# Layer 1's flag product ahead of the last chunk, transposed scores paired to 512 columns, GpSimd given a third tile, and 128-row scores in layer 0

## The chip, the cores and the metric

One core of one Trainium2 chip runs the whole program in one launch. The metric is the device time in microseconds, the median of several runs. Beside it stands one execution taken with the hardware profiler, whose lines are shown here. Line numbers such as L1502 are lines of the kernel before.

## The reference

Two transformer layers on an input of 2 batches x 1024 tokens x 128 features. Each normalizes the rows and then adds an attention and a feed-forward part to its input:

```python
xn = layernorm(x); x = x + attn0(xn) + ffn0(xn)      # layer 0
xn = layernorm(x); x = x + attn1(xn) + ffn1(xn)      # layer 1
```

`attn0` has 16 heads of 8 features, with biases, causal mask and softmax. `ffn0` is a mixture of 8 experts with the best two chosen. `ffn1` walks 8 decision trees of depth 7. `attn1` has 16 query heads and 4 key heads of 64 features, with rotary positions, causal mask and a choice of the 64 largest scores of each row:

```python
scores = einsum('bhqd,bhkd->bhqk', q, k) / 8; scores = where(future, -1e30, scores)
threshold = top_k(scores, 64)[0][..., -1:]
weights = softmax(where(scores < threshold, -1e30, scores))
out = einsum('bhqk,bhkd->bhqd', weights, v) @ Wo.T
```

## The kernel before

The program runs stage after stage: projections of layer 0, its attention (`attend_layer0`, about 80 to 547 us), its experts, projections of layer 1, the trees, and layer 1's attention (`attend_layer1`, from about 1215 us to the end). Each stage has a block of code for every engine, and semaphores order them. The order of the work on each engine is written out by hand. P is 128, S is 1024 rows of a batch, TB = 8 tiles of 128 rows, and CH = 512 columns.

**Layer 0, one head (32 of them, software pipelined).** For a stable softmax the kernel first needs each row's peak. `row_unit` computes scores row by row (line 350, operands of 64 rows, and a mask of 128 rows, line 353) in 12 units of at most 512 columns into two buffers; VectorE reduces each unit to a maximum (line 463) and makes from the maxima three bf16 parts of a shift (lines 466 to 472). TensorE turns the shift (line 394), ScalarE copies it into rows 64 to 66 of `q` (line 439), where `k` holds ones. Then the scores are computed again with keys on the partitions (line 407, 128 rows, with a mask, line 410), one tile of keys at a time, ScalarE takes the exponential (line 445), and `pv` multiplies by the values of the head before (line 374). ScalarE copies that product (`oT`, line 451) behind the exponential of tile 5, and TensorE transposes it into the row buffers (line 424). `rows_ahead(count)` issues row units of the next head between these steps: two at first, then 2, 1, 2, 1, 1, ... behind each tile of keys. GpSimd copies values (`values`).

**Layer 1, one section.** A section n works on several heads at once: it computes the scores of head n+1, counts in head n, sorts head n-1, weighs head n-2 and leaves head n-3. The sections n = 4 to 27 run as six turns of a loop of four; the others are written out.
- TensorE, `scores`: a tile of 128 rows against all its keys in fp32 (line 1208) and a mask (line 1210). VectorE's `keep_scores(j)` copies it to SBUF with its peak (line 1463). `TILE` turns j into the tile, the widest first: j = 0 is 1024 columns, j = 7 is 128.
- ScalarE, `count`: three times, it counts the scores above a trial value in every tile (line 1332). Between them VectorE works out the next trial from the count in small steps (`first_move`, ends in line 1548; `second_move`, ends in line 1581). They are split by `yield`, so that other work is put between the steps.
- VectorE, `tally` and `split_tally` (lines 1421 to 1430): from the three counts, a value `found` slightly above the threshold. `mark(i)` keeps of tile i what lies below it (line 1436, two SBUF inputs). GpSimd does this for tiles 7 and 6 by a comparison (line 1307) and a product (line 1312), `EARLY = 2`. `sort(i, 0..2)` takes the sixteen largest of what is left by three passes (lines 1448, 1450, 1452). Behind the sorting, eight small steps make the threshold, and a `verdict` whether the search failed somewhere in the head.
- The flag: TensorE sums the verdict over the partitions (line 1260), VectorE copies it (`flags`, line 1470), loads it into a register and branches (`judge`); behind that it writes the `cutoff` (line 1502). Where the flag is set the head's tiles are sorted in full.
- ScalarE, `gate` (line 1342): per tile, a large number where a score lies under the cut-off. TensorE, `turn` (lines 1224, 1226): a chunk of up to four 128x128 blocks is transposed and the gate subtracted, into one of two buffers. ScalarE, `weights` (line 1351): the exponential of the chunk. TensorE, `weigh` (line 1237): times the values.
- ScalarE copies the sum (`copy_out`, line 1358), TensorE projects it (`project`, line 1249), VectorE divides and adds it to `x` (`shares`, line 1510, and `leave`, line 1519).

The lines of the flag on TensorE stand at the head of a section, behind all chunks of the section before:

```python
if gating:
    pe.wait_ge(verdict_ready, n - 1)
    wait(pe, t_read, (n - 2) * TU)
    pe.matmul(ps_flag, g.ones[:, 0:1], verdict[:, :], start=True, stop=True).then_inc(flag_back, 1)
```

## Time and profile before

| what | value |
|---|---|
| time, median of 3 runs | 2691.27 us (2687.34 to 2691.73) |
| the profiled execution's own time | 2691.92 us |
| its span in the profile | 2689.9 us |
| mean granted clock of TensorE | 0.858 of full speed |
| busy: TensorE, VectorE, ScalarE, GpSimd | 77%, 64%, 53%, 15% |
| TensorE's weight loads | 43% |

The span runs from the first to the last instruction; the time has 2.0 us more around it. Busy shares are means over stages that differ, so they don't say what bounds one stage. The granted clock has two levels, 1.2 GHz (0.5) and 2.4 GHz (1.0).

### The profile page before, as it was taken

What the parts mean: (1) busy time and instruction counts of PE and PEld (TensorE: products, weight loads), DVE (VectorE), ACT (ScalarE), POOL (GpSimd) and SP (SyncE); (2) the same over time, 40 slices, a digit from 0 to 9 for tenths busy, and PEclk for the clock granted to TensorE, in tenths of its full rate; (3) what the DMA queues carried; (4) which work ended last, traced back from release to release, by engine and by line L of the source; (5) the groups of instructions that cost most, each with busy time, mean ns of one, the idle gap of its engine ahead of it and who ended that gap; (6) DMA issues with size and microseconds to landing.
All of it is one profiled execution on the core that took longest, in us unless ns stands there. A gap on an engine that the chain in (4) does not pass through costs nothing. (4 is left out here: it accounts for less than half of the span.)

```text
span 2689.9 us, 36464 instructions
## 1 busy us (share of the span) xinstructions
PE 2060.2 (77%) x10416; PEld 1158.8 (43%) x10448; DVE 1710.9 (64%) x4622; ACT 1415.4 (53%) x2979; POOL 393.6 (15%) x262
## 2 busy tenths in 40 slices
PE   6799999899988968885676777777767567767766
PEld 4233333377764435552343444444434334434434
DVE  4556656521125666765886777777777777877784
ACT  2344444444324213324766666666666566766673
POOL 0000000000012400001212121222212212221211
PEclk7699999999968969997788878788888778888877
DMA  6000000000011200001000000000000000000000
GB/s 179 18 16 15 15 15 15 8 28 1 0 39 55 88 15 0 0 5 44 21 13 25 13 25 12 25 12 24 14 24 17 20 12 18 19 24 12 17 5 21
DMA packets 38267, 62.43 MB, mean 23 GB/s; under 512 B 10226, under 2 KB 15348, under 8 KB 38005
## 3 DMA queue, kind: packets, MB, share of 16 engines
q1 hardware_dynamic: 38069, 60.51, 7.7%
q14 instruction: 161, 1.31, 0.2%
q8 instruction: 37, 0.61, 0.1%
HBM read 34.14 MB, written 17.83 MB: 19 GB/s over the span
## 5 line engine op out<-in xcount | busy, mean ns | idle before, releaser
L1332 ACT ACTIVATE a_trash<-a_sc,a_search 128x1024 bf16<-128x1024 f32 (+7 forms) x768 | 585.7, 766 | 294.2 <-DVE a_search L1581 164.4
L1237 PE MATMUL a_ps_o<-a_kT,a_v 128*65 128x512 f32 (+3 forms) x768 | 376.8, 584 | 214.8 <-ACT a_kT L1351 213.6
L1208 PE MATMUL a_ps_s<-a_k,a_q 128*128 128x512 f32 (+3 forms) x768 | 343.5, 562 | 141.5 <-DVE a_sc L1463 128.1
L1307 POOL TENSOR_SCALAR a_below<-a_sc,a_found 128x1024 f32<-128x1024 f32 x64 | 171.9, 2686 | 1103.5 <-POOLq L1303 1103.5
L1224 PE MATMUL a_ps_t<-g_ident,a_sc 128*128 128x128 f32 x1152 | 298.2, 331 | 33.4 <-ACT a_short L1342 33.3
L463 DVE TENSOR_REDUCE a_top<-a_ps_row 128x1 f32<-128x512 f32 (+3 forms) x384 | 207.4, 557 | 161.4 <-PE a_ps_row L353 107.6
L1226 PE MATMUL a_ps_t<-a_minus,a_short 128*128 128x128 bf16 x1152 | 268.0, 253 | 0.0
L1224 PEld LDWEIGHTS a_ps_t<-g_ident,a_sc 128*128 128x128 f32 x1152 | 199.2, 173 | 154.9 <-issue 92.0
L1351 ACT ACTIVATE a_kT<-a_ps_t 128x512 f32<-128x512 f32 (+3 forms) x384 | 184.6, 481 | 118.8 <-PE a_ps_t L1226 115.0
L1208 PEld LDWEIGHTS a_ps_s<-a_k,a_q 128*128 128x128 f32 x768 | 142.2, 214 | 235.9 <-DVE a_sc L1463 140.5
L445 ACT ACTIVATE a_prob<-a_ps_col 128x1024 f32<-128x1024 f32 (+7 forms) x256 | 158.3, 653 | 147.2 <-PE a_ps_col L407 113.0
L1342 ACT ACTIVATE a_short<-a_sc,a_cutoff 128x1024 bf16<-128x1024 f32 (+7 forms) x256 | 177.0, 764 | 95.3 <-DVE a_cutoff L1502 95.1
L1463 DVE TENSOR_SCALAR_CACHE_REDUCE a_sc<-a_ps_s,g_search 128x1024 f32<-128x1024 f32 (+7 forms) x256 | 207.2, 809 | 24.6 <-PE a_ps_s L1210 9.0
L1237 PEld LDWEIGHTS a_ps_o<-a_kT,a_v 128*65 128x65 f32 x768 | 88.7, 158 | 285.6 <-ACT a_kT L1351 238.0
L1448 DVE MAX8 a_sorted<-a_below 128x8 f32<-128x768 f32 (+7 forms) x256 | 192.8, 754 | 1.2
L1452 DVE MAX8 a_sorted<-a_below 128x8 f32<-128x768 f32 (+7 forms) x256 | 192.5, 752 | 0.0
L1450 DVE MATCH_REPLACE8 a_below<-a_sorted,a_below 128x768 f32<-128x768 f32 (+7 forms) x256 | 189.5, 742 | 0.0
L1226 PEld LDWEIGHTS a_ps_t<-a_minus,a_short 128*128 128x128 bf16 x1152 | 139.8, 121 | 91.6 <-issue 91.5
L584 ACT ACTIVATE ex_hid<-ex_ps_h,le_b 128x512 f32<-128x512 f32 x128 | 87.8, 687 | 128.5 <-PE ex_ps_h L561 128.1
L1332 ACT ACTIVATION_READ_ACCUMULATOR a_trash<-a_sc,a_search 128x1 f32 x768 | 147.0, 191 | 0.0
L350 PE MATMUL a_ps_row<-a_k,a_q 64*128 64x512 bf16 (+3 forms) x384 | 132.5, 346 | 13.9 <-DMA a_k<-stack 12.7
L1312 POOL TENSOR_TENSOR a_below<-a_sc,a_below 128x1024 f32<-128x1024 f32 x64 | 142.4, 2225 | 2.8
(244 smaller groups left out, 3218.3 us busy)
## 6 DMA issues: line engine op xcount, KB each, us to landing
a_v<-g_v SPq DMA_DIRECT2D x32, 260.0 KB, 2.3
q1turned<-p_full SPq DMA_DIRECT2D x32, 256.0 KB, 2.0
a_q<-q1turned SPq DMA_DIRECT2D x32, 256.0 KB, 3.6
a_k<-k1turned SPq DMA_DIRECT2D x32, 256.0 KB, 4.1
stack<-p_parts SPq DMA_DIRECT2D x24, 256.0 KB, 3.8
a_q<-stack SPq DMA_DIRECT2D x32, 96.0 KB, 2.2
a_k<-stack SPq DMA_DIRECT2D x32, 96.0 KB, 2.2
le_w<-d_w SPq DMA_DIRECT2D x1, 2048.0 KB, 8.9
```

What stands on the lines that cost most here:

```text
L463: m = dve.tensor_reduce(top[:, i, c:c + 1], ps_row[:, u % 2, 0:width], AX.X, ALU.max)
L1208: pe.matmul(ps_s[:, j % 2, c:c + w], q[:, p, i * P:width], k[:, p, c:c + w], start=True, stop=True)
L1224: pe.matmul(out, columns(h, i)[:, c * P:(c + 1) * P], g.ident[:, :], is_transpose=True, start=True, stop=False)
L1226: m = pe.matmul(out, short[:, OFF[i] + c * P:OFF[i] + (c + 1) * P], minus[:, :], start=False, stop=True)
L1237: m = pe.matmul(ps_o[0:VW1, lo // HALF, (lo % HALF) * P:CH], v[:, p, c, :], kT[:, x % 2, 0:(hi - lo) * P], start=(c == 0), stop=(c == hi - 1))
L1332: act.activation(trash[:, u % 2, 0:(i + 1) * P], columns(h, i), ACT.Sign, scale=-1.0, bias=trials[:, p, c, i:i + 1], accum_out=balance[:, ...
L1342: act.activation(short[:, OFF[i]:OFF[i] + (i + 1) * P], columns(h, i), ACT.Relu, scale=-STEEP, bias=cutoff[:, h % 2, i:i + 1]).then_inc(ga ...
L1351: act.activation(kT[:, x % 2, 0:w], ps_t[:, x % 2, 0:w], ACT.Exp).then_inc(t_read, 1)
L1448: m = dve.max(sorted_[:, i, 0:8], buf)
L1450: m = dve.match_replace(buf, sorted_[:, i, 0:8], buf, -3.0e38)
L1452: m = dve.max(sorted_[:, i, 8:16], buf)
L1463: dve.tensor_scalar(columns(h + 1, i), ps_s[:, j % 2, 0:(i + 1) * P], shift.rearrange("p n i -> p (n i)"), None, ALU.subtract, ALU.max, ac ...
```

## The change

In layer 0, the row scores take all 128 rows of `q` and `k` instead of the first 64. Since rows 64 to 66 of `q` hold an old shift by then, GpSimd clears them behind each head's last columns (`clear`, 1024 columns of three partitions), and TensorE waits for it. Behind every tile of keys two row units are issued, so that the twelve end with tile 4, before its `pv`.

In layer 1:
- The product of the flag moves from the head of section n+1 to the end of section n, ahead of the last `weigh`, and to the buffer that is free there.
- The 12 chunks become 9 of 512 columns: narrow pieces are put together, and their order changes. The gates are made all in one go, the small tiles first.
- TensorE's scores j = 4 to 7 of the next head are issued behind chunks 0, 1, 3 and 5 instead of 0, 1, 2 and 3, the two of the head after that behind chunks 6 and 7. `scores(7)` so stands behind `weigh(5)` and `turn(7)`.
- `EARLY = 3`: GpSimd marks tile 5 too.
- VectorE's order: the first two kept scores and `mark(4)` come between tally and flag, `mark(3)` between the flag and its branch, `mark(2)` behind the cut-off; tile 5 is sorted last, tiles 7, 6, 1 and 0 earlier, and `keep_scores(7)` comes behind `sort(5, 0)`.

```diff
@@ attend_layer0
+                def clear(n, h):
+                    pool.wait_ge(v_ready, n + 2)
+                    pool.wait_ge(col_ready, n * CU + CU)
+                    pool.tensor_tensor(q[SHIFT0:SHIFT0 + NSH, h, :], none[SHIFT0:SHIFT0 + NSH, :],
+                                       none[SHIFT0:SHIFT0 + NSH, :], ALU.add).then_inc(cleared, 1)
+                    pool.wait_ge(cleared, n + 1)
...
-                with pool.Fori(1, NH // 2) as i:
-                    values(i * 2, 0)
-                    values(i * 2 + 1, 1)
+                with pool.Fori(1, NH // NQ) as i:
+                    for h in range(NQ):
+                        clear(i * NQ + (h - 2), (h + 2) % NQ)
+                        values(i * NQ + h, h % 2)
...
+                        wait(pe, cleared, i4 * NQ + (h - NQ + 1))
...
-                    last = pe.matmul(ps_row[:, u % 2, 0:width], q[0:SHIFT0, h, i * P:(i + 1) * P],
-                                     k[0:SHIFT0, h, c * CH:c * CH + width], start=True, stop=True)
+                    last = pe.matmul(ps_row[:, u % 2, 0:width], q[:, h, i * P:(i + 1) * P],
+                                     k[:, h, c * CH:c * CH + width], start=True, stop=True)
...
-                        rows_ahead(2 if j in (0, 2) else 1)
+                        rows_ahead(2)
...
+                dve.memset(none[:, :], 0.0)
@@ attend_layer1
-        EARLY = 2
+        EARLY = 3
...
-        CHUNKS = [(c, max(c, lo), lo + HALF) for lo in (HALF, 0) for c in range(lo + HALF)]
+        CHUNKS = ([((0, 0, 4),), ((1, 1, 4), (3, 3, 4))] + [((c, HALF, TB),) for c in range(5)]
+                  + [((5, 5, 8), (7, 7, 8)), ((6, 6, 8), (2, 2, 4))])
+        NARROW = 2
+        LAST = (2, 6)
+        GATES = [0, 1, 2, 3, 7, 6, 5, 4]
...
@@ TensorE
-                    if gating:
-                        pe.wait_ge(verdict_ready, n - 1)
-                        wait(pe, t_read, (n - 2) * TU)
-                        pe.matmul(ps_flag, g.ones[:, 0:1], verdict[:, :], start=True, stop=True).then_inc(flag_back, 1)
...
                     for x in range(TU):
+                        if sorting and x == TU - 1:
+                            pe.wait_ge(verdict_ready, n)
+                            pe.matmul(ps_t[0:1, 1 - odd, 0:TB + 1], g.ones[:, 0:1], verdict[:, :], start=True,
+                                      stop=True).then_inc(flag_back, 1)
                         if gating:
-                            weigh(n - 2, i4 * 2 + h // 2 - 1, h % 2, x)
+                            weigh(n - 2, i4 * 2 + h // 2 - 1, h % 2, odd + x, x)
                             if x + 2 < TU:
-                                turn(n - 2, h + 2, x + 2)
-                        if ahead and x < HALF:
-                            scores(n + 1, i2, p1, HALF + x)
-                        if late and x in (9, 11):
-                            scores(n + 2, i4 * 2 + (h + 2) // 2, 1 - p1, x // 2 - 4)
+                                turn(n - 2, h + 2, odd + x, x + 2)
+                        if ahead and x in (0, 1, 3, 5):
+                            scores(n + 1, i2, p1, HALF + (x + 1) // 2)
+                        if late and x in (6, 7):
+                            scores(n + 2, i4 * 2 + (h + 2) // 2, 1 - p1, x - 6)
@@ ScalarE
-                        if leaving and s == 1:
+                        if leaving and s == 2:
                             copy_out(n - 3)
                     if gating:
-                        for j in range(HALF):
+                        for j in range(TB):
                             gate(n - 2, h + 2, j)
...
-                            weights(n - 2, s // 2)
-                    if gating:
-                        for j in range(HALF, TB):
-                            gate(n - 2, h + 2, j)
-                        weights(n - 2, HALF)
+                            weights(n - 2, odd + s // 2, s // 2)
+                    if gating:
+                        weights(n - 2, odd + HALF, HALF)
...
-                            weights(n - 2, HALF + 1 + s // 2)
-                    if gating:
-                        for x in range(2 * HALF + 1, TU):
-                            weights(n - 2, x)
+                            weights(n - 2, odd + HALF + 1 + s // 2, HALF + 1 + s // 2)
```

VectorE's order in a full section after the change, `next` being one step of a move:

```python
tally; split_tally; keep_scores(0), (1); mark(4); flags; mark(3); judge; cut_off
next(first); mark(2); next(first); shares(0); next(first); shares(1); leave(0)
rest of first; leave(1); keep_scores(2); mark(1); sort(4,0); mark(0); sort(3,0), (4,1), (3,1)
shares(2); leave(2); keep_scores(3); sort(4,2), (2,0), (3,2), (2,1), (7,0), (2,2); keep_scores(4)
sort(7,1), (1,0), (7,2), (1,1), (6,0); next(second); sort(6,1); next(second); keep_scores(5)
next(second); sort(1,2); next(second); sort(0,0); next(second); sort(0,1); next(second); sort(0,2)
rest of second (line 1581); keep_scores(6); sort(6,2), (5,0); keep_scores(7); sort(5,1); hit; sort(5,2)
eight small steps to the verdict
```

## Rows read from the trace of the kernel before

**Rows 1.** Layer 1's attention: busy us (instructions) by engine, clock, DMA
```profile
1215.00:2690.00 1475.00, 1019.77 (x4672) 587.31 (x4672) 1096.15 (x3186) 962.90 (x2241) 317.05 (x158) 0.82 0.07 18
```

**Rows 2.** Groups by line, 1379.5 to 2089.4 us; then all of line 439
```profile
L1502 DVE SCALAR_TENSOR_TENSOR a_cutoff<-a_thr,a_ceiling 128x8 f32<-128x8 f32 x16 | 2.9, 179 | 38.5 <-issue 38.5
...
L439 ACT ACTIVATE a_q<-a_ps_col x32: 1012/1012/1012, 92.2 to 520.1; 3x1024 bf16<-3x1024 f32 x32
```

**Rows 3.** VectorE's timeline, layer 1: start, duration, what, [idle before <-releaser]
```profile
1723.41 0.18 DVE L1421 TENSOR_TENSOR a_above<-a_wide,a_balance 128x24 f32<-128x24 f32 x1 [2.96 <-remote]
...
1728.66 0.15 DVE L1470 TENSOR_SCALAR a_flag<-a_ps_t 1x1 int32<-1x1 f32 x1 [4.24 <-PE a_ps_t L1260]
...
1757.59 0.16 DVE L1581 SCALAR_TENSOR_TENSOR a_search<-a_fac,a_search 128x8 f32<-128x8 f32 x1
...
1765.42 0.18 DVE L1421 TENSOR_TENSOR a_above<-a_wide,a_balance 128x24 f32<-128x24 f32 x1
...
1771.93 0.15 DVE L1470 TENSOR_SCALAR a_flag<-a_ps_t 1x1 int32<-1x1 f32 x1 [5.50 <-PE a_ps_t L1260]
1772.38 1.28 DVE L1463 TENSOR_SCALAR_CACHE_REDUCE a_sc<-a_ps_s,g_search 128x1024 f32<-128x1024 f32 x1 [0.31 <-issue]
...
1773.93 1.15 DVE L1463 TENSOR_SCALAR_CACHE_REDUCE a_sc<-a_ps_s,g_search 128x896 f32<-128x896 f32 x1 [0.26 <-DVE a_sc L1463]
...
1777.42 0.17 DVE L1502 SCALAR_TENSOR_TENSOR a_cutoff<-a_thr,a_ceiling 128x8 f32<-128x8 f32 x1 [2.33 <-issue]
```

**Rows 4.** Groups of VectorE by line and shape in layer 1, 1400 to 2400 us
```profile
L1450 DVE MATCH_REPLACE8 a_below<-a_sorted,a_below 128x1024 f32<-128x1024 f32 x23 | 27.8, 1209 | 0.0
...
L1436 DVE SCALAR_TENSOR_TENSOR a_below<-a_sc,a_found 128x768 f32<-128x768 f32 x22 | 22.2, 1010 | 0.0
```

**Rows 5.** Timeline of ScalarE in the same section of layer 1
```profile
1757.86 1.15 ACT L1332 ACTIVATE a_trash<-a_sc,a_search 128x1024 bf16<-128x1024 f32 x1 [5.19 <-DVE a_search L1581]
...
1760.04 0.47 ACT L1351 ACTIVATE a_kT<-a_ps_t 128x384 f32<-128x384 f32 x1
...
1764.65 0.20 ACT L1332 ACTIVATION_READ_ACCUMULATOR a_trash<-a_sc,a_search 128x1 f32 x1
```

**Rows 6.** TensorE's timeline, layer 1; last, a stretch with its clock (0.58)
```profile
1787.66 1.44 PE L1237 MATMUL a_ps_o<-a_kT,a_v 128*65 128x512 f32 x2 [4.59 <-ACT a_kT L1351]
...
1790.17 1.82 PE L1208 MATMUL a_ps_s<-a_k,a_q 128*128 128x512 f32 x2
...
1799.55 0.49 PE L1208 MATMUL a_ps_s<-a_k,a_q 128*128 128x128 f32 x2 [1.75 <-DVE a_sc L1463]
...
1787.60:1791.50 3.90, 3.84 (x12) 1.96 (x13) 3.87 (x10) 3.90 (x11) 0.00 (x0) 0.58 0.00 0
```

**Rows 7.** GpSimd's timeline, behind the tally of 1765.42
```profile
1766.62 2.84 POOL L1307 TENSOR_SCALAR a_below<-a_sc,a_found 128x1024 f32<-128x1024 f32 x1 [32.02 <-POOLq L1303]
...
1769.58 2.35 POOL L1312 TENSOR_TENSOR a_below<-a_sc,a_below 128x1024 f32<-128x1024 f32 x1
```

**Rows 8.** Timelines at 1297 us; all of line 1502, ns min/median/max
```profile
1297.48 2.34 DVE L1436 SCALAR_TENSOR_TENSOR a_below<-a_sc,a_found 128x640 f32<-128x640 f32 x1
...
1297.07 2.08 POOL L1312 TENSOR_TENSOR a_below<-a_sc,a_below 128x896 f32<-128x896 f32 x1
...
L1502 DVE SCALAR_TENSOR_TENSOR a_cutoff<-a_thr,a_ceiling x32: 166/168/686, 1294.4 to 2658.3; 128x8 f32<-128x8 f32 x32
```

**Rows 9.** Timeline of TensorE in one head of layer 0
```profile
303.72 0.39 PE L350 MATMUL a_ps_row<-a_k,a_q 64*128 64x512 bf16 x1
304.04 0.23 PE L353 MATMUL a_ps_row<-g_maskq,g_identb 128*128 128x128 bf16 x1
...
305.20 0.39 PE L407 MATMUL a_ps_col<-a_q,a_k 128*128 128x512 bf16 x1
305.43 0.22 PE L410 MATMUL a_ps_col<-g_maskk,g_identb 128*128 128x128 bf16 x1
```

**Rows 10.** Groups by line and shape in layer 0, 110 to 520 us
```profile
L463 DVE TENSOR_REDUCE a_top<-a_ps_row 128x1 f32<-128x512 f32 x180 | 124.5, 692 | 47.3 <-PE a_ps_row L350 44.0 <-PE a_ps_row L353 0.4
```

More of the change, by code:

```diff
@@ L1212, in scores, with turn, weigh @@
                     m.then_inc(s_ready, 1)
[L1214 to L1216 removed]
+                def turn(n, h, u, x):
                     if x == 0:
                         pe.wait_ge(gated, n * TB + HALF)
[L1219 removed]
+                    if x == NARROW:
                         pe.wait_ge(gated, n * TB + TB)
                     wait(pe, t_read, n * TU + (x - 1))
[L1222 to L1227 removed]
+                    a = 0
+                    for c, lo, hi in CHUNKS[x]:
+                        for i in range(lo, hi):
+                            out = ps_t[:, u % 2, a * P:(a + 1) * P]
+                            pe.matmul(out, columns(h, i)[:, c * P:(c + 1) * P], g.ident[:, :], is_transpose=True,
+                                      start=True, stop=False)
+                            m = pe.matmul(out, short[:, OFF[i] + c * P:OFF[i] + (c + 1) * P], minus[:, :],
+                                          start=False, stop=True)
+                            a += 1
                     m.then_inc(t_ready, 1)
[L1230 to L1232 removed]
+                def weigh(n, n2, p, u, x):
                     if x == 0:
@@ L1252, in section @@
                 def section(n, i4, h):
-                    ahead, _, _, gating, leaving = parts_of(n)
+                    ahead, _, sorting, gating, leaving = parts_of(n)
                     late = not isinstance(n, int) or n + 2 < NH
@@ L1469, in flags @@
                         dve.wait_ge(flag_back, n - 1)
-                        return did(dve.tensor_scalar(flag[:, TB:TB + 1], ps_flag[:, TB:TB + 1], float(TB * P), None, ALU.add))
+                        return did(dve.tensor_scalar(flag[:, TB:TB + 1], ps_t[0:1, p, TB:TB + 1], float(TB * P), None, ALU.add))
                     def do_again(i):
@@ L1492, in judge @@
                             dve.sem_clear(redo)
-                            Chain(dve, redo)(dve.tensor_scalar(flag[:, 0:TB], ps_flag[:, 0:TB], float(P), None, ALU.add))
+                            Chain(dve, redo)(dve.tensor_scalar(flag[:, 0:TB], ps_t[0:1, p, 0:TB], float(P), None, ALU.add))
                             do_again(0)
@@ L1594, in section @@
                         keep_scores(1)
+                    if sorting:
+                        mark(4)
+                    if gating:
+                        flagged = flags()
+                    if sorting:
+                        mark(3)
                     if gating:
@@ L1598, in section @@
                         cut_off()
+                    next(first, None)
+                    if sorting:
+                        mark(2)
+                    next(first, None)
                     if leaving:
                         shares(0)
+                    next(first, None)
+                    if leaving:
                         shares(1)
                         leave(0)
+                    for _ in first:
+                        pass
+                    if leaving:
                         leave(1)
-                    if sorting:
-                        mark(5)
-                    next(first, None)
                     if ahead:
                         keep_scores(2)
-                    next(first, None)
                     if sorting:
-                        mark(4)
-                    next(first, None)
-                    if sorting:
-                        mark(3)
-                    next(first, None)
+                        mark(1)
+                        sort(4, 0)
+                        mark(0)
+                        sort(3, 0)
+                        sort(4, 1)
+                        sort(3, 1)
                     if leaving:
@@ L1618, in section @@
                         leave(2)
-                    if sorting:
-                        mark(2)
-                        sort(5, 0)
-                        mark(1)
-                        sort(4, 0)
-                        mark(0)
-                    for _ in first:
-                        pass
-                    if sorting:
-                        sort(5, 1)
-                        sort(4, 1)
                     if ahead:
@@ L1651, in section @@
                     if sorting:
-                        sort(2, 2)
-                    next(second, None)
-                    if sorting:
-                        sort(1, 0)
+                        sort(1, 2)
                     next(second, None)
@@ L1660, in section @@
                     if sorting:
-                        sort(1, 1)
+                        sort(0, 1)
+                    next(second, None)
+                    if sorting:
+                        sort(0, 2)
                     for _ in second:
                         pass
-                    if sorting:
-                        sort(7, 2)
                     if ahead:
```

72 lines of the change are left out of this document (34 added, 38 removed).

## The prediction

> **What bounds the kernel now.** I read first what the busy times of layer 1's attention say: it takes 1475 of 2690 us, and no engine fills it; VectorE, the fullest, has 1096 us, TensorE 1020 [rows 1]. The groups of lines then give the rhythm: 16 sections (heads) of layer 1 in 709.9 us, 44.4 us each, and 32 heads of layer 0 at (520.1 - 92.2) / 31 = 13.8 us, mostly 13.5 [rows 2].
>
> What closes the loop in layer 1 is in VectorE's timeline. It tallies a head at 1765.42, and then stands 5.5 us for the flag's product (4.24 in the section before, beside a 2.96 us loop branch) [rows 3]. TensorE issues that product only after the last chunks and two large scores, and those chunks wait for ScalarE's third count, which starts 0.27 us after VectorE's second move (line 1581) [rows 3, 5]. So the ring is: flag to second move, 1728.66 to 1757.59 = 28.9 us of VectorE's own work, then 1757.59 to 1771.93 = 14.3 us through ScalarE and TensorE; 43.3 us, and about 1 us more a section from loop branches.
>
> **Layer 1, the new ring.** With the product ahead of the last `weigh`, VectorE meets no wait after the tally. Time from tally (T) to the second move, starting from the 28.9:
> - the flag stood 0.45 ahead of the first kept score [rows 3]; now tally and split come first (1.0, the row of line 1307 starting 1.20 after the tally shows when `found` is out [rows 3, 7]) and 0.45 of registers: +1.0;
> - `mark(5)` goes to GpSimd: -1.05 [rows 4];
> - tile 5's three passes move behind the second move: 3 x 0.9, -2.7; ahead of it come the third pass of tile 7 (1.15), two of tile 6 (2.1), and small passes of tiles 1 and 0 (0.35 and 0.5): +4.1. The passes of 1024 columns are 1.21 [rows 4], the others are scaled by width, less 0.07 of overlap;
> - kept score to cut-off is 1777.42 - 1773.93 = 3.49 [rows 3], of which the kept score covered 1.15; `mark(3)` (0.75) covers less: +0.5 with the flag's copy.
> Sum 28.9 + 1.0 - 1.05 - 2.7 + 4.1 + 0.5 = 30.8; I carry 30.9.
>
> From the second move to the next tally, before: 7.8 [rows 3]. Now `keep_scores(7)` stands there, and score 7 is issued after `weigh(5)` and `turn(7)`. `weigh(5)` needs ScalarE's fifth-indexed weights, after two counts: 1760.04 - 1757.59 = 2.45 [rows 3, 5], 0.6 for a chunk of 512, then `weigh` and `turn` of four tiles, 1790.17 - 1787.66 = 2.5 at the clock's lower level [rows 6], and a score of 128 columns, 0.8 after its start (0.49 at the upper level [rows 6]). That is 6.4 after the move; VectorE's own work in between is 2.4, so a new stall of about 4. Behind it stand `sort(5,1)`, `hit`, `sort(5,2)` and the eight small steps to the next tally (0.3 + 0.9 + 0.2 + 1.0 + 1.8 = 4.2). Total 10.6. TensorE will be at the lower level there: it has been idle some 7 us by then, and after a shorter idle of 4.6 us the granted clock was 0.58 over the next 3.9 us [rows 6].
>
> ScalarE's counts end 1764.85 - 1757.59 = 7.3 after the move [rows 3, 5], 8.1 with four chunks of 512 between: under 10.6, so the stall for score 7 covers them. The product itself is out about 2 to 3 us after T (TensorE does two large scores first), and VectorE asks at 4.8: covered, by 2 us. Without that cover its wait comes back. Pairing 12 chunks to 9 changes no column and saves ScalarE three short instructions, hidden; so are the eight gates in one go, since by my count the second tally that VectorE asks for is then complete at T + 22 and asked for at T + 27.
>
> The loop branch of 2.96 [rows 3] now lies wholly on VectorE's path: 0.73 a section. For moments at which TensorE's two large scores run at the lower clock I add 0.35.
> Section: 30.9 + 10.6 + 0.73 + 0.35 = 42.6, a gain of 1.8 on 44.4, if VectorE runs undisturbed.
>
> **What GpSimd's third tile costs.** Before, nearly all marks run after GpSimd is done. Where they do meet, a mark of 128x640 took 2.34 us, more than twice one of 128x768 (1.01), and ended 0.67 after GpSimd's TENSOR_TENSOR; the cut-off, ordinarily 0.17, took up to 0.69 in such a spot [rows 4, 8]. I read that as: a VectorE instruction with two SBUF inputs stands until GpSimd's TENSOR_TENSOR ends. The Trainium skill (GPSIMD Engine Reference, Key points) says the same, that the engines share SBUF interfaces and contend for VectorE instructions with two SBUF inputs; by that rule the new order pays, without it the gain of 1.8 stands.
>
> GpSimd's times after T are 1.2 to 4.0 compare, 4.2 to 6.5 multiply [rows 7], then compare and multiply to 11.2, and for tile 5 (scaled to 768 columns) compare to 13.4, multiply to 15.3. VectorE: `mark(4)` at 4.1, `mark(3)` 4.9, cut-off 8.4, `mark(2)` 8.7, line 1545 at 9.7, line 1548 at 11.1, `mark(1)` 14.1, `mark(0)` 15.2. If `mark(4)` gets in 0.1 us ahead of the first multiply, GpSimd shifts by 0.7; `mark(3)` then stands, but the branch before the cut-off hides that; line 1548 or 1545 stands 0.85 to 2.1, `mark(1)` or `mark(0)` 0.9 to 1.3: 2.0 to 2.9, taken 2.3. All lie ahead of the second move, on the ring. Section 44.9, +0.5. About 30 sections run in full: +15 us. The first and last sections, and the one redo, I cost at nothing: same work.
>
> **Layer 0.** At 512 columns, a 64-row score takes 304.04 - 303.72 = 0.32 to the next instruction, a 128-row one 305.43 - 305.20 = 0.23 [rows 9]. So each change between 64 and 128 rows costs 0.09 to 0.10; 12 row units have 24 of them, 2.3 us a head. Most of it isn't kept. `rows_ahead(2)` puts all twelve units ahead of the third `pv`, at the rate at which VectorE reduces (0.69 for 512 columns [rows 10]): I count 1.2 us of new waits at tiles 2 and 4. The third `pv`, and with it tile 5's columns and the copy of `oT`, come at nearly their old place in the head, and the transposes that follow set its end. Kept 0.4 a head, 31 x 0.4 = 12 us; bounds 0.3 lost and 1.4 kept. GpSimd's `clear` has no row; by its 1024-column instruction [rows 7] it takes 2.3, below that 0.25 if three partitions were cheap. It starts after the head's last columns and GpSimd is otherwise idle; uncovered, it would hold VectorE's shift and cost up to 0.8 a head. The extra memset is 0.5 us, once.
> The Trainium skill (TensorE: Matmul & The Clock Gate, Part 3) says a weight load overlaps a running matmul only if its row group differs. By that, 128 rows throughout would expose every load and layer 0 would gain nothing, 12 us more in the sum. The rows of 128 rows disagree: 0.23 us for 512 columns leaves a load no room [rows 9].
>
> **Sum.** Own time of the profiled execution 2691.9 (span 2689.9 plus 2.0): +15 - 12 + 0.5 = 2695.4; it lies 0.6 above the runs' median, so 2695.
>
> **Rivals.**
> 1. No contention worth naming (few cases in the trace; the races fall well). 30 x -1.8 = -54, -12: 2626. For it: marks beside GpSimd's compare ran at their usual time. Against: the 2.34 us mark. It decides from a loss under 1.8 a section. Chance 0.27.
> 2. `mark(4)` loses the race for GpSimd's first multiply: it stands 2.4, the branch and the cut-off start that much later, line 1548 still meets a multiply. 4.0 lost a section, +2.2 x 30 = +66, -12: 2746. The two arrive within 0.1 us. Chance 0.20.
> 3. TensorE at its upper clock after the wait (5.2 in place of 6.4), or layer 0 keeping over 1 us a head: 2655 to 2675. Chance 0.08. Layer 0's `clear` on VectorE's path: 2720, chance 0.02. Layer 0 giving nothing at all, because the gap of 0.09 us isn't one of rows: 2707, inside the forecast, 0.05 of its chance; the two gaps at equal width speak against it [rows 9].
> The forecast (2675 to 2715) has 0.43.
>
> **Chances.** 0.2% is 5.4 us, about what can be told from no change. The forecast's own range gives 0.11 faster, 0.12 same, 0.20 slower. With the rivals: faster 0.27 + 0.07 + 0.11 = 0.45, same 0.13, slower 0.42. To hold 8 in 10 the range takes in rivals 1 and 2: 2620 to 2750.
>
> **What the profile would show.** Right: no wait of line 1470; about 4 us of idle before `keep_scores(7)`, put down to TensorE; two-input VectorE instructions stretched where GpSimd multiplies; sections of 44 to 46 us. Marks at their old means and sections of 42.6 mean rival 1; a `mark(4)` of 3 us means rival 2. In layer 0, row scores 0.23 apart at 512 columns and heads near 13.1. I am wrong if the stall before `keep_scores(7)` isn't there, or if contention hits the sorting passes too.

## Result, and the profile after

The changed kernel takes 2763.59 us (median of 4 runs, 2762.1 to 2765.5) against 2691.45 for the kernel before: ratio 1.0272, 95% interval 1.0254 to 1.0290. It is slower, by 70.2 us between the two profiled executions (2762.1 and 2691.9), and outside the predicted range. Among the runs below one execution of `both`, 4619.5 us where its nine others took 2682 to 2689, is left out.

Where it goes is seen from three rows. The first is all of the line that copies layer 0's shift rows, once a head (line 439 before, [rows 2]); the second all of layer 1's kept scores; the third the row of layer 1's attention that answers to [rows 1].

```profile
L455 ACT ACTIVATE a_q<-a_ps_col x32: 1012/1012/1012, 91.5 to 501.3; 3x1024 bf16<-3x1024 f32 x32
...
L1481 DVE TENSOR_SCALAR_CACHE_REDUCE a_sc<-a_ps_s,g_search x256: 334/810/1286, 1199.9 to 2650.8; 128x1024 f32<-128x1024 f32 x32, 128x768 f32<-128x768 f32 x32, 128x512 f32<-128x512 f32 x32, 128x256 f32<-128x256 f32 x32
...
1190.70:2760.20 1569.50, 1029.71 (x4672) 594.99 (x4672) 1226.41 (x3154) 950.28 (x2145) 464.80 (x222) 0.77 0.06 17
```

Layer 0 gained: its 32 heads run from 91.5 to 501.3, 409.8 us in place of 427.9 [rows 2]. Layer 1 lost more than that: its kept scores take 1450.9 us from first to last, 95.3 more than before (1224.3 to 2579.9 there). In the third row VectorE is busy for 1226 us, 130 more than in [rows 1], although the change moved work from it to GpSimd, whose busy time rose from 317 to 465.

VectorE's timeline shows one section of it, as [rows 3] does for before. It starts with the kept score of the smallest tile, at the end of the section before. Columns: start, duration, what, and in brackets the idle time before it and its releaser.

```profile
1872.44 0.35 DVE L1481 TENSOR_SCALAR_CACHE_REDUCE a_sc<-a_ps_s,g_search 128x128 f32<-128x128 f32 x1 [4.53 <-PE a_ps_s L1228]
...
1876.63 0.18 DVE L1439 TENSOR_TENSOR a_above<-a_wide,a_balance 128x24 f32<-128x24 f32 x1
...
1880.73 3.09 DVE L1454 SCALAR_TENSOR_TENSOR a_below<-a_sc,a_found 128x640 f32<-128x640 f32 x1
1883.75 0.14 DVE L1488 TENSOR_SCALAR a_flag<-a_ps_t 1x1 int32<-1x1 f32 x1
1883.82 1.43 DVE L1454 SCALAR_TENSOR_TENSOR a_below<-a_sc,a_found 128x512 f32<-128x512 f32 x1
1887.60 0.80 DVE L1520 SCALAR_TENSOR_TENSOR a_cutoff<-a_thr,a_ceiling 128x8 f32<-128x8 f32 x1 [2.35 <-issue]
...
1888.39 1.27 DVE L1454 SCALAR_TENSOR_TENSOR a_below<-a_sc,a_found 128x384 f32<-128x384 f32 x1
...
1891.41 1.06 DVE L1566 SCALAR_TENSOR_TENSOR a_search<-a_fac,a_search 128x8 f32<-128x8 f32 x1
```

And GpSimd's timeline of the same section:

```profile
1880.79 2.36 POOL L1336 TENSOR_TENSOR a_below<-a_sc,a_below 128x1024 f32<-128x1024 f32 x1
1883.13 3.09 POOL L1331 TENSOR_SCALAR a_below<-a_sc,a_found 128x896 f32<-128x896 f32 x1
1886.30 2.07 POOL L1336 TENSOR_TENSOR a_below<-a_sc,a_below 128x896 f32<-128x896 f32 x1
1888.35 2.20 POOL L1331 TENSOR_SCALAR a_below<-a_sc,a_found 128x768 f32<-128x768 f32 x1
1890.63 1.81 POOL L1336 TENSOR_TENSOR a_below<-a_sc,a_below 128x768 f32<-128x768 f32 x1
```

The wait for the flag is gone: line 1488 has no idle time before it. In its place the instructions of VectorE that read two operands from SBUF and lie beside GpSimd's multiplies are long. `mark(4)`, 640 columns, starts 0.06 us ahead of the multiply and ends 0.67 behind it; the cut-off of 8 columns ends 0.03 behind the second multiply, line 1566 0.03 behind the third. Kept scores, which read PSUM, keep their duration. `keep_scores(7)` has the new wait that the prediction speaks of, 4.53 us.

To compare runs I take the same numbers from each trace: from VectorE's tally (T) to its next one, over the full sections between about 1400 and 2620 us (23 to 26 of them, without the one that is redone; which of the last sections are counted moves a mean by up to 0.3), and in it T to the flag, T to the cut-off, T to the second move, and second move to next tally. "Excess" is, summed over VectorE's instructions of a section, what each takes above its usual time, that of the same line and shape in early0, where GpSimd marks nothing, so that early0 has 0.00 by definition. "Branch" is from the end of the branch ahead of the cut-off to the cut-off's start. All are means in us.

```
kernel       section  flag   cut-off  2nd move  rest   excess  branch
before        44.23   6.75   12.26    35.82      8.41   0.04    2.80
changed       47.67   6.99   10.73    35.98     11.69   5.12    2.89
early0        45.91   4.84    9.43    34.12     11.79   0.00    3.54
early2        45.92   6.87   10.64    34.16     11.77   3.53    2.84
late          47.65   4.07    8.69    36.01     11.65   2.97    3.67
late_dl       46.40   4.06    7.69    34.96     11.43   2.95    2.67
sc7           44.06   7.12   11.48    35.79      8.27   2.96    3.45
both          44.45   5.42    9.37    36.17      8.28   2.62    3.06
sc7_dl        43.81   7.24   10.85    35.56      8.25   3.07    2.75
sc7_e2_dl     42.51   7.20   10.77    34.07      8.44   2.03    2.72
best          41.40   7.04   10.59    32.96      8.44   1.69    2.69
flag          43.11   4.78   11.50    34.72      8.39   0.09    3.98
```

### The profile page after: what moved, and what is told of

Same layout as the page of the kernel before. It is cut to its first block and busy times, and to the rows that moved or that the text cites. A ratio compares the mean times of both kernels' runs of the same rounds, so it can differ in the third digit from the quotient of the medians.

```text
span 2760.2 us, 36380 instructions
## 1 busy us (share of the span) xinstructions
PE 2007.9 (73%) x10448; PEld 1154.2 (42%) x10448; DVE 1837.0 (67%) x4591; ACT 1403.8 (51%) x2883; POOL 600.3 (22%) x356
## 5 line engine op out<-in xcount | busy, mean ns | idle before, releaser
L1331 POOL TENSOR_SCALAR a_below<-a_sc,a_found 128x1024 f32<-128x1024 f32 (+2 forms) x96 | 257.8, 2686 | 1054.6 <-POOLq L1327 1054.6
L1373 ACT ACTIVATE a_kT<-a_ps_t 128x512 f32<-128x512 f32 x288 | 169.0, 587 | 227.8 <-PE a_ps_t L1245 227.8
L1272 PE MATMUL a_ps_o<-a_wo,a_oT 65*128 (+1 forms) x512 | 94.6, 339 | 237.1 <-DVE g_x L1537 231.9
L479 DVE TENSOR_REDUCE a_top<-a_ps_row 128x1 f32<-128x512 f32 (+3 forms) x384 | 196.7, 553 | 94.4 <-PE a_ps_row L366 60.6
L1366 ACT ACTIVATE a_short<-a_sc,a_cutoff 128x128 bf16<-128x128 f32 (+7 forms) x256 | 174.0, 762 | 159.7 <-DVE a_cutoff L1520 159.7
L1336 POOL TENSOR_TENSOR a_below<-a_sc,a_below 128x1024 f32<-128x1024 f32 (+2 forms) x96 | 203.4, 2119 | 5.5
L1466 DVE MAX8 a_sorted<-a_below 128x8 f32<-128x640 f32 (+7 forms) x256 | 193.1, 754 | 3.3
L1470 DVE MAX8 a_sorted<-a_below 128x8 f32<-128x640 f32 (+7 forms) x256 | 192.2, 751 | 0.0
L1454 DVE SCALAR_TENSOR_TENSOR a_below<-a_sc,a_found 128x640 f32<-128x640 f32 (+4 forms) x160 | 191.2, 1197 | 0.1
L1468 DVE MATCH_REPLACE8 a_below<-a_sorted,a_below 128x640 f32<-128x640 f32 (+7 forms) x256 | 189.5, 742 | 0.0
L1272 PEld LDWEIGHTS a_ps_o<-a_wo,a_oT 65*128 65x128 f32 x512 | 79.4, 236 | 253.3 <-DVE g_x L1537 239.6
```

The costliest lines, as they stand in the source:

```text
L479: m = dve.tensor_reduce(top[:, i, c:c + 1], ps_row[:, u % 2, 0:width], AX.X, ALU.max)
L1331: pool.tensor_scalar(lows(i), columns(h - 1, i), found[:, i:i + 1], None, ALU.is_le).then_inc(kinds, 1)
L1336: pool.tensor_tensor(lows(i), columns(h - 1, i), lows(i), ALU.mult).then_inc(marked, 1)
L1454: lane[i] = did(dve.scalar_tensor_tensor(lows(i), columns(hs, i), found[:, i:i + 1], columns(hs, i), ALU.is_le, ALU.mult))
L1466: m = dve.max(sorted_[:, i, 0:8], buf)
L1470: m = dve.max(sorted_[:, i, 8:16], buf)
```

## Experiments

The time of the kernel before, measured beside each, was 2686.5 us (l0, late, sc7, both), 2688.6 (early0, early2, flag, late_dl) and 2687.6 (the other four); ratios are against it, with 95% intervals.

**l0**: layer 0 of the changed kernel, layer 1 of the one before.

> The kernel before with the changed layer 0 alone, layer 1 as before. The changed kernel's trace has layer 0 at 13.2 us a head in place of 13.5, with first head to last 409.8 us in place of 427.9. Theory A (layer 0 gains about what was forecast, all of the loss is layer 1's): 2691 - 12 to - 18, 2673 to 2680 us. Rival (layer 0 gains nothing of its own and ran faster for another reason): 2691. If layer 0's change disturbs layer 1 or another stage: above 2691.

Measured 2665.16 us, ratio 0.9917 (0.9901 to 0.9934). Layer 0 is a gain by itself; all of the loss is layer 1's.

**l0rows**: the same with the places of the early row scores as before.

```diff
-                        rows_ahead(2)
+                        rows_ahead(2 if j in (0, 2) else 1)
```

> The kernel before with layer 0's 128-row scores alone: the places at which row scores are issued ahead stay as before (two, one, two, one in place of two each time), layer 1 as before. The whole layer-0 part took 21 us off (ratio 0.9917), where 12 were forecast. Theory A (the gain is that of the row switches, 24 a head, most of it hidden behind VectorE): 0.985 of the way, 2688 - 15 to 21 = 2667 to 2673 us. Rival (the gain is from issuing the scores earlier): 2685 to 2688 us.

Measured 2679.10 us, ratio 0.9968 (0.9956 to 0.9980). Neither: the 128-row scores alone give 8.5 us, less than half. The first and last copy of the shift rows stand in the two traces (l0, then l0rows) at:

```profile
L455 ACT ACTIVATE a_q<-a_ps_col x32: 1011/1011/1012, 90.5 to 501.1; 3x1024 bf16<-3x1024 f32 x32
```

```profile
L455 ACT ACTIVATE a_q<-a_ps_col x32: 1012/1012/1012, 90.9 to 511.7; 3x1024 bf16<-3x1024 f32 x32
```

410.6 and 420.8 us against 427.9: 7.1 us come from the rows, 10.2 from issuing the scores earlier once the rows are there. Earlier scores with the rows as before weren't run.

**early0**: GpSimd marks nothing and only copies the start values (that part of its block isn't shown), VectorE marks tiles 7, 6 and 5 too.

```diff
-        EARLY = 3
+        EARLY = 0
...
+                        mark(7)
                         sort(7, 0)
...
+                        mark(6)
                         sort(6, 0)
...
+                        mark(5)
                         sort(5, 0)
```

> The changed kernel with GpSimd marking no tile: VectorE marks tiles 7, 6 and 5 as well, each right ahead of its first sorting pass; GpSimd only copies the start values. VectorE gets 3.5 us of work more a section, of which mark(5) lies in the wait before keep_scores(7). Theory A (GpSimd's work costs VectorE 5.1 us a section before the second move): 5.1 goes, 2.4 comes: section 47.7 - 2.7 = 45.0, 2763 - 81 = 2682 us. Rival (no contention, the long instructions have another cause such as the order): 2763 + 30 x 2.4 = 2835 us.

Measured 2717.12 us, ratio 1.0109 (1.0092 to 1.0126): faster than the changed kernel by 46 us though VectorE has 3.4 us of work more in each section, so the rival is out. Groups of VectorE's marks by shape and the cut-off, over 1362.6 to 2129.9 us, first of the changed kernel, then of early0 (busy us, mean ns):

```profile
L1454 DVE SCALAR_TENSOR_TENSOR a_below<-a_sc,a_found 128x640 f32<-128x640 f32 x16 | 49.4, 3088 | 0.0
L1454 DVE SCALAR_TENSOR_TENSOR a_below<-a_sc,a_found 128x512 f32<-128x512 f32 x16 | 22.8, 1425 | 0.0
L1454 DVE SCALAR_TENSOR_TENSOR a_below<-a_sc,a_found 128x384 f32<-128x384 f32 x16 | 20.3, 1266 | 0.0
...
L1520 DVE SCALAR_TENSOR_TENSOR a_cutoff<-a_thr,a_ceiling 128x8 f32<-128x8 f32 x17 | 15.9, 938 | 37.6 <-issue 37.6
```

```profile
L1446 DVE SCALAR_TENSOR_TENSOR a_below<-a_sc,a_found 128x640 f32<-128x640 f32 x16 | 14.1, 879 | 0.0
L1446 DVE SCALAR_TENSOR_TENSOR a_below<-a_sc,a_found 128x512 f32<-128x512 f32 x16 | 11.7, 729 | 0.0
L1446 DVE SCALAR_TENSOR_TENSOR a_below<-a_sc,a_found 128x384 f32<-128x384 f32 x17 | 10.4, 611 | 0.0
...
L1512 DVE SCALAR_TENSOR_TENSOR a_cutoff<-a_thr,a_ceiling 128x8 f32<-128x8 f32 x17 | 2.8, 167 | 63.0 <-issue 63.0
```

With GpSimd's work gone, the three marks and the cut-off, which stand where they did in VectorE's order, take about half of the time or less. The gain was 1.8 a section and not the expected 2.7 because the idle time ahead of the cut-off rose (63.0 us of 17 against 37.6): `mark(3)`, no longer stretched, covers less of the branch, and the branch itself takes longer (3.54 against 2.89), on which more below.

**early2**: GpSimd marks two tiles, VectorE tile 5 (`EARLY = 2`, `mark(5)` ahead of `sort(5, 0)`).

> The changed kernel with GpSimd marking two tiles as before and VectorE marking tile 5 in the wait before keep_scores(7). Theory A (the excess of each two-input instruction belongs to the GpSimd instruction beside it): what stood beside GpSimd's tile 5 (line 1566, 0.85, and part of mark(2), 0.63) goes, mark(4) and mark(3) still stand: 0.9 to 1.5 a section, 2718 to 2737 us. Rival (the third tile is what the whole 5.1 us comes from): 2763 - 30 x 4 = 2640 us. Rival 2 (no effect of GpSimd): 2763 us.

Measured 2713.77 us, ratio 1.0093 (1.0077 to 1.0110), a little more than was expected. The excess falls from 5.12 to 3.53, and idle time ahead of the second move by some 0.3: the third tile is worth a third of the contention, not all of it. The mark of 640 columns still takes 3085 ns.

**late**: VectorE's marks of tiles 4, 3 and 2 behind `keep_scores(2)`, taken out of their places ahead of it.

```diff
                     if sorting:
+                        mark(4)
+                        mark(3)
+                        mark(2)
                         mark(1)
```

> The changed kernel with VectorE's marks of tiles 4, 3 and 2 moved behind keep_scores(2), in front of mark(1), so that nearly all of GpSimd's work on its three tiles is over when they start. No instruction is added or dropped. Theory A (VectorE's two-input instructions stand beside GpSimd's work, about 5 us a section in the changed kernel): most of it goes, some stays because GpSimd is at work until 15.8 us after the tally and the moved marks start at about 11: section 44 to 45.5, 2763 - 30 x 2.5 to 3.5 = 2660 to 2690 us. Rival (the loss comes from the order of the passes and new waits, not from contention): no change or slower, 2755 to 2790.

Measured 2765.93 us, ratio 1.0300 (1.0277 to 1.0323). A miss: no gain. It doesn't speak for the rival, though. VectorE, then GpSimd, in the section at 1781:

```profile
1785.74 0.14 DVE L1488 TENSOR_SCALAR a_flag<-a_ps_t 1x1 int32<-1x1 f32 x1
1790.55 0.17 DVE L1520 SCALAR_TENSOR_TENSOR a_cutoff<-a_thr,a_ceiling 128x8 f32<-128x8 f32 x1 [4.67 <-issue]
1790.78 2.06 DVE L1544 TENSOR_TENSOR a_reach<-a_wide_aim,a_balance 128x8 f32<-128x8 f32 x1
...
1795.24 1.67 DVE L1571 TENSOR_TENSOR a_gap<-a_search 128x8 f32<-128x8 f32 x1 [0.15 <-DVEq L1429]
...
1798.55 2.46 DVE L1454 SCALAR_TENSOR_TENSOR a_below<-a_sc,a_found 128x640 f32<-128x640 f32 x4
```

```profile
1790.74 2.08 POOL L1336 TENSOR_TENSOR a_below<-a_sc,a_below 128x896 f32<-128x896 f32 x1
...
1795.08 1.81 POOL L1336 TENSOR_TENSOR a_below<-a_sc,a_below 128x768 f32<-128x768 f32 x1
```

In this section the marks run at their usual time, four of them in 2.46 us; in 7 of 16 sections `mark(4)` still stands, 1.36 to 2.22 us. And steps of 8 columns stand in their place, 2.06 us where their usual time is 0.15: what counts is that a multiply is running, not the size of the VectorE instruction. The excess fell by 2.15, and nearly as much came back as idle time ahead of the cut-off (from 3.8 to 6.0 a section, summed from the tally on): no mark covers the branch, and the branch takes 3.67 in place of 2.89.

**late_dl**: the same, the loads of v, q and k held back until the first move.

```diff
                         sp.wait_ge(pv_done, (i * 2 + p - 1) * TU)
+                        sp.wait_ge(moved, (i * 2 + p + 1) * (COUNTS - 1) + 1)
```

> The changed kernel with late marks (the run of 2766 us) and one wait more on SyncE: the loads of v, q and k that go out at the start of a section wait for VectorE's first move, so that they are issued some 8 us later. In the run with late marks VectorE stood 3.7 us in the mean after the branch ahead of the cut-off (2.7 to 4.5) against 2.85 in the changed kernel, and there the loads were issued 0 to 2 us ahead of the branch, in the changed kernel 2.5 to 4.5 ahead. Theory A (the instruction fetch behind the branch stands behind the loads on the DMA engines): the stand becomes 2.7, 1.0 a section, 2766 - 30 = 2736 us. Rival (the loads have nothing to do with it): 2766 us and 3.7 us. If the later loads come too late for scores: slower.

Measured 2742.30 us, ratio 1.0207 (1.0186 to 1.0228), 24 us less than late. The branch came down from 3.67 to 2.67, the excess stayed (2.97 and 2.95). SyncE's queue in the trace of late, one set of loads, and below it how long such a load takes to land and the queue that carries instructions, from the views of DMA issues and queues:

```profile
1785.34 0.52 SPq L1186 DMA_DIRECT2D a_v<-g_v  x1
1786.14 0.47 SPq L1180 DMA_DIRECT2D a_q<-q1turned  x1
1786.83 0.47 SPq L1181 DMA_DIRECT2D a_k<-k1turned  x1
...
q14 instruction: 8, 0.07, 0.2%
...
a_k<-k1turned SPq DMA_DIRECT2D x2, 256.0 KB, 4.0
```

VectorE copies the flag at 1785.74 in late, so the loads are in flight during the branch. In the trace of late the last load goes out at least 2.4 us ahead of the branch's end in 5 of 23 sections, and there the branch takes 2.69 to 2.98; in the others 2.97 to 4.52. In the loop of the changed kernel the last load is 2.3 to 5.8 us ahead. That the loads lengthen the branch is shown by the one edit, which holds them back and nothing else. That what stands behind them is the fetch of the code behind the branch is my reading of queue q14, not shown.

**sc7**: score 7 behind chunk 4.

```diff
-                        if ahead and x in (0, 1, 3, 5):
-                            scores(n + 1, i2, p1, HALF + (x + 1) // 2)
+                        if ahead and x in (0, 1, 3, 4):
+                            scores(n + 1, i2, p1, HALF + (0, 1, 3, 4).index(x))
```

> The changed kernel with the score of the last tile (score 7) issued by TensorE behind chunk 4 in place of chunk 5, that is before the chunk that waits for ScalarE's counts after VectorE's second move. Theory A (the wait of 4.5 us before keep_scores(7) is on the ring): it goes, and ScalarE's counts, which end 7.7 to 8 us after the second move, bound the next tally in its place: second move to tally 11.3 becomes about 8.2, 2763 - 30 x 3.1 = 2670 us. Rival (the wait is filled by another at once, as VectorE's flag or score 4 come later): 2740 to 2765.

Measured 2671.74 us, ratio 0.9938 (0.9921 to 0.9954): 92 us less than the changed kernel, as expected, and faster than before. From the second move to the next tally 11.69 became 8.27. VectorE's timeline around one tally:

```profile
1790.23 0.18 DVE L1439 TENSOR_TENSOR a_above<-a_wide,a_balance 128x24 f32<-128x24 f32 x1 [1.26 <-ACT a_trash L1356]
...
1795.49 1.15 DVE L1481 TENSOR_SCALAR_CACHE_REDUCE a_sc<-a_ps_s,g_search 128x896 f32<-128x896 f32 x1 [1.12 <-PE a_ps_s L1228]
...
1796.57 0.88 DVE L1454 SCALAR_TENSOR_TENSOR a_below<-a_sc,a_found 128x640 f32<-128x640 f32 x1
```

ScalarE's last count now bounds the tally, and VectorE comes early enough to wait for the two large scores (1.31 and 0.97 in the mean). By that wait `mark(4)` starts later, well inside the multiply or behind it, and stands for less of it: 0.88 in this section and from 0.88 to 3.07 in the 17 of the window, where it was 3.06 to 3.10 in the changed kernel (excess 2.96 in place of 5.12). The wait has taken the place of the excess, and the second move comes hardly earlier behind the tally (35.79).

**both**: late marks and sc7 together.

> Both edits together, late marks and score 7 behind chunk 4. If both waits are on the ring and independent: the two gains add, 2763 - 85 - 93 = 2585 us, section near 41. Rival (with VectorE quicker, TensorE's flag product or ScalarE's gates and counts bound the section): 2630 to 2660, less than the sum of the two.

Measured 2685.02 us, ratio 0.9995 (0.9985 to 1.0005), 13 us slower than sc7 alone: a miss against both expectations. After late's result it is what I would expect, since late marks had given nothing there either; no run takes the 13 us apart.

**sc7_dl**: sc7 with the loads held back.

> The changed kernel with score 7 behind chunk 4 (2672 us) and the loads of v, q and k delayed until VectorE's first move. Stand behind the branch in the run without the delay 3.45 us in the mean, with the delay in the late-marks kernel 2.67. Theory A (the fetch stands behind the loads): 0.8 a section, 2672 - 24 = 2648 us. Rival (that gain was special to the late marks): 2672 us.

Measured 2666.08 us, ratio 0.9916 (0.9897 to 0.9935): 6 us, not 24. The branch fell from 3.45 to 2.75 as expected, the cut-off came 0.63 earlier and the second move only 0.23: what was won ahead of the cut-off was mostly lost again behind it, where the small steps stood longer beside the multiplies (the first move's last step, line 1566 of the changed kernel, has 0.83 in excess, the cut-off 0.55).

**sc7_e2_dl**: that, and GpSimd with two tiles; VectorE marks tile 5 ahead of `sort(5, 0)`, where it stood for the last count.

> As before, and GpSimd marks two tiles only, VectorE marks tile 5 after the second move, where it stood 1.3 us for the last count. Theory A: contention falls from about 3.0 to 1.5 to 2 a section and mark(5) fits in the slack: 2648 - 30 x 1.2 = 2612 us. Rival (with less contention VectorE only waits longer for the two large scores in keep_scores(0) and (1)): 2640 to 2650 us.

Measured 2628.12 us, ratio 0.9779 (0.9763 to 0.9794): 38 us, as theory A has it (36; its 2612 us started from 2648). The excess fell from 3.07 to 2.03.

**best**: that, and all five marks of VectorE directly behind the tally.

```diff
                         split_tally()
+                        for i in (4, 3, 2, 1, 0):
+                            mark(i)
                     if ahead:
                         keep_scores(0)
```

> As the one before, and all five of VectorE's own first marks (tiles 4 to 0, 3.0 us) directly behind the split tally, ahead of keep_scores(0): they lie in the time in which VectorE stood for the large scores (2.3 us) and end about when GpSimd's first multiply starts, 4.0 after the tally. Theory A (waits and contention are both filled): section 1.5 to 2.8 shorter than in the run before, 2530 to 2570 us. Rival (the branch, no longer covered by a mark, and the small two-input steps of the first move, which now stand beside GpSimd, give it back): 2600 to 2615 us.

Measured 2594.31 us, ratio 0.9654 (0.9639 to 0.9669): faster than both kernels, and between the two expectations. The section is 1.1 shorter, less than theory A has.

```profile
1801.26 0.18 DVE L1440 TENSOR_TENSOR a_above<-a_wide,a_balance 128x24 f32<-128x24 f32 x1 [0.35 <-ACT a_trash L1357]
...
1802.30 3.60 DVE L1455 SCALAR_TENSOR_TENSOR a_below<-a_sc,a_found 128x640 f32<-128x640 f32 x5
...
1808.43 0.14 DVE L1489 TENSOR_SCALAR a_flag<-a_ps_t 1x1 int32<-1x1 f32 x1
1812.02 1.02 DVE L1521 SCALAR_TENSOR_TENSOR a_cutoff<-a_thr,a_ceiling 128x8 f32<-128x8 f32 x1 [3.44 <-issue]
```

The marks fill the time in which VectorE stood for the large scores; the kept scores, which read PSUM, lie beside the end of the compare and the first multiply and lose nothing. Of the five marks, all beside GpSimd's compare, `mark(3)` alone is long, 1.6 us in place of 0.73. The 3.44 us ahead of the cut-off, with nothing to cover them, and the cut-off's 0.75 of excess are the part of the rival that came true.

**flag**: the kernel before with the product alone moved ahead of TensorE's last `weigh`.

```diff
+                        if sorting and x == TU - 1:
+                            pe.wait_ge(verdict_ready, n)
+                            pe.matmul(ps_flag, g.ones[:, 0:1], verdict[:, :], start=True, stop=True).then_inc(flag_back, 1)
                         if gating:
```

> The kernel before with one edit: TensorE issues the flag's product ahead of its last weigh of a section in place of at the start of the next one; VectorE's order, GpSimd's two tiles, the chunks and layer 0 stay. Theory A (the 5.8 us wait for the flag, 16 sections of the trace, is on the ring and nothing takes its place): section 44.2 - 5 = 39, 2686 - 150 = 2536 us. Rival, held likelier (the two large scores, which come just ahead of the product, are late too, and VectorE waits for them in keep_scores(0) and keep_scores(1) instead, as it does for 3 us where score 7 comes earlier): gain 0.5 to 2 a section, 2626 to 2671 us.

Measured 2667.48 us, ratio 0.9945 (0.9917 to 0.9972), in the rival's range. T to flag went from 6.75 to 4.78 only: TensorE reaches the product late. In the section whose tally is at 1801.41 it is at the last chunks until 1804.5, then comes a large score and only then the product:

```profile
1804.50 1.94 PE L1208 MATMUL a_ps_s<-a_k,a_q 128*128 128x512 f32 x4
1806.33 0.60 PE L1237 MATMUL a_ps_o<-a_kT,a_v 128*65 128x256 f32 x2
1806.86 0.20 PE L1276 MATMUL a_ps_t<-a_verdict,g_ones 128*1 128x9 f32 x2
```

And the branch takes 3.98 in place of 2.80: the last load goes out 0.5 to 0.9 us ahead of its end in the loop, where it was 2.6 to 2.9 before. My reason, that the large scores are late too, was half right: the first large score holds up the product itself; the second one is done just as VectorE asks for it, so `keep_scores(1)` waits no longer than before.

## Why the prediction was wrong

**Bound and ring: right.** In before the loop is closed by flag, second move, third count and last chunks. Moving the product took the wait away, though the run flag shows that the move alone doesn't: there the product starts 5.45 us after the tally, in the changed kernel 2.10 ("2 to 3" was said), and VectorE, which now does other work first, asks at 7.1. How much of that is VectorE's order and how much TensorE's new chunks no run separates.

```profile
1878.73 0.20 PE L1300 MATMUL a_ps_t<-a_verdict,g_ones 128*1 128x9 f32 x2
```

**T to the second move without contention: right.** Predicted 30.9; measured 35.98 less an excess of 5.12, 30.9. That takes the whole excess to be on the path. Early0 gives a check: 34.12 less 2.4 for the marks of tiles 7 and 6 is 31.7, of which 0.65 is its longer branch.

**Second move to next tally: right, a little small.** Predicted 10.6 and 0.73 for the loop branch, 11.3; measured 11.69. The score came 7.1 after the move, whose last step is below, where 6.4 was said (1865.33 to 1872.44). The prediction called the new wait of about 4 us, measured 4.24 in the mean, but set it against the wait it replaced and went on. sc7 shows what it was worth: the one edit that takes it away turns a loss of 2.7% into a gain of 0.6%, nearly all of it between second move and tally (11.69 to 8.27).

```profile
1865.33 0.15 DVE L1599 SCALAR_TENSOR_TENSOR a_search<-a_fac,a_search 128x8 f32<-128x8 f32 x1
```

**The step that failed: "2.0 to 2.9, taken 2.3", what GpSimd's third tile costs.** The mechanism was right, the size was 5.12. Three things are in it. First, the race of `mark(4)` for the first multiply, which I gave to rival 2 with a chance of 0.20. The times were forecast well, 4.1 and 4.2 after the tally; in the section shown they are 4.10 and 4.16. But a lead of 0.06 didn't win: `mark(4)` stood for the whole multiply (3.09 us) in all 24 sections of the loop (mean 3088 ns where 879 is usual, 2.2 a section). In the 8 sections that are written out it comes earlier and takes its 0.88. There `mark(3)` starts ahead of the multiply, and GpSimd is the one that loses, its multiply taking 2.84 to 2.91 in place of 2.36 in six of them:

```profile
2525.47 0.88 DVE L1454 SCALAR_TENSOR_TENSOR a_below<-a_sc,a_found 128x640 f32<-128x640 f32 x1
2526.34 0.73 DVE L1454 SCALAR_TENSOR_TENSOR a_below<-a_sc,a_found 128x512 f32<-128x512 f32 x1
```

```profile
2526.38 2.91 POOL L1336 TENSOR_TENSOR a_below<-a_sc,a_below 128x1024 f32<-128x1024 f32 x1
```

What decides when the two start within 0.1 us isn't shown; giving the better side the larger chance was a bet without a reason.

Second, rival 2 said 4.0 and 2746 us, still too little: `mark(3)` and `mark(2)` lose 0.66 and 0.63 beside a compare. The prediction has it that marks beside a compare keep their usual time. The trace of before had two that did (at 1261.77 and 1262.60) and one that didn't, which I overlooked, 768 columns in 1.77 us where 1.01 is usual [rows 4]:

```profile
1294.51 1.77 DVE L1436 SCALAR_TENSOR_TENSOR a_below<-a_sc,a_found 128x768 f32<-128x768 f32 x1
```

Third, the cut-off (0.75) and line 1566 (0.85) stand. Of these the prediction had line 1566 (there line 1548), and beside it `mark(1)` or `mark(0)`, which lose under 0.1. Early0 shows that it is GpSimd's work that makes all of these instructions long.

The 2.8 that were missing and 0.36 in the rest, less the 0.35 that the prediction added for TensorE's clock and that no row shows apart, make 2.8 a section. From tally to tally the 24 sections of the loop lost 83.5 us together, 3.5 each where 0.5 was forecast: that is 71 of the 80 us by which layer 1 missed (95.3 measured against 15). The other 9 lie in the sections that are written out, and there I didn't take them apart.

**Contention and the sorting passes: right.** None of their lines has an excess above 0.02.

**A wait that I missed.** `weigh(0)` of TensorE waits for the last `leave`, which the new order puts 21.7 us behind the tally; score 4 comes late and `keep_scores(4)` waits, 0.63 in the section shown and 0.52 in the mean. The rows are TensorE's and VectorE's of that section:

```profile
1899.08 1.96 PE L1259 MATMUL a_ps_o<-a_kT,a_v 128*65 128x512 f32 x2 [3.74 <-DVE g_x L1537]
```

```profile
1904.41 0.75 DVE L1481 TENSOR_SCALAR_CACHE_REDUCE a_sc<-a_ps_s,g_search 128x512 f32<-128x512 f32 x1 [0.63 <-PE a_ps_s L1228]
```

**Layer 0: right in sign, small by a third.** 12 us forecast, 18.1 in the trace (17.3 in that of l0). Of the two parts the row switches gave less than I kept for both (7.1), and the earlier scores, for which I had counted 1.2 us of new waits a head, gave 10.2. `clear` takes 1.89 us (2.3 was estimated), and neither it nor the memset costs anything that shows. Layer 1 starts 24.4 us earlier (1199.9 against 1224.3), 6 more than the heads of layer 0 explain; where they come from I haven't taken apart.

**Rival 1** (no contention) is out by early0. **Rival 3** is out too: the granted clock was 0.50 over the 3.9 us from 1867.8, the lower level, and layer 0 kept 0.6 us a head and not over 1.

## What to carry to other kernels

Work that is moved to GpSimd isn't free for VectorE: before giving it a tile, list which VectorE instructions with two SBUF operands fall beside it, small ones too, and put there what reads PSUM or waits anyway. Here GpSimd's work cost VectorE 5.1 us a section in one order, and 1.7 in another that left GpSimd one tile less. When two estimates differ by less than their error, take the worse side for the forecast or give both equal weight. And a wait that you find while adding up the new order is a thing to remove, even where the sum still comes out even: one index in the order of scores was worth 92 us here.

## What the runs showed of the hardware

- A VectorE instruction with two SBUF operands that starts while GpSimd multiplies two SBUF operands doesn't end before the multiply, whatever its size. In the thirteen traces in which GpSimd marks tiles (all but early0) 683 marks, cut-offs and steps of a move start so in layer 1, and none ends before the multiply; 8 columns took up to 2.1 us in place of 0.15. The sorting passes, which read one operand, and kept scores and `leave`, which read PSUM, end at their usual time. The Trainium skill (GPSIMD Engine Reference, Key points) says that the two engines share SBUF interfaces and contend for such instructions; the trace agrees, and gives the price.
- The multiply itself keeps its time where VectorE stands (2.36 us beside `mark(4)`, 2.35 in [rows 7]). It is the longer one, 2.84 to 2.91, where VectorE's marks were under way first. A lead of 0.06 us wasn't enough for `mark(4)`.
- Beside GpSimd's compare a mark can be long, and the compare too: 512 columns took 1.43 in place of 0.73, the compare of 896 columns 3.09 in place of 2.52 (late). It isn't always so: of the five marks beside the compare in best one was long, and in before two kept 0.83 and 0.74. What decides it isn't shown.
- A taken branch over code that isn't executed costs VectorE 2.7 us until the next instruction, and up to 4.5 if 0.8 MB of loads are in flight (late); holding the loads back brought the mean from 3.67 to 2.67.
